# The residual of the Mamba stage: summed by DVE, or added by PE in the output projection's bank and copied by ACT

## The reference, cut to what matters

```
for i in range(4):                      # layers
    h = _rms(x, norm_w[i])
    xi, z = split(h @ W_in[i].T)        # 512 channels each
    xc = silu(conv4(xi) + conv_b[i])
    delta, Bm, Cm = split(xc @ W_x[i].T)
    delta = softplus(delta @ W_dt[i].T + b_dt[i])
    hs = scan(exp(delta * A), delta * xc * Bm)        # along the 512 tokens, 16 states
    y = sum_n(hs * Cm) + D[i] * xc
    out = (y * silu(z)) @ W_out[i].T                  # 512 x 256 a batch
    x = x + out                                       # the residual
```

## Time and profile before

| | |
|---|---|
| median of 3 runs | 4388.03 us (4382.81 to 4389.73) |
| the profiled execution's own time | 4372.04 us |
| its span | 4370.3 us |
| PE, DVE, ACT, POOL busy in the span | 85%, 70%, 53%, 54% |
| mean granted TensorE clock | 0.903 |
| Mamba stage, first product to last scan | 1796.4 to 3680.1 us |

### The profile page before, as it was taken

One profiled execution on the slowest core, in us unless ns is written; L12 is line 12 of the kernel. 1 busy time (PEld: TensorE's weight loads), 2 busy tenths in 40 slices (PEclk: granted clock), 3 DMA queues, 4 the chain that ended last, 5 costly groups with the idle time before them and its releaser, 6 DMA issues. The chain is left out here.

```text
span 4370.3 us, 51349 instructions
## 1 busy us (share of the span) xinstructions
PE 3704.9 (85%) x16520; PEld 1775.5 (41%) x16528; DVE 3046.8 (70%) x4067; ACT 2338.0 (53%) x4238; POOL 2360.4 (54%) x1238
## 2 busy tenths in 40 slices
PE   7979889889779995789898888899888977887786
PEld 3444444445369993222222222222222212454453
DVE  3566557556631113599999999999999997546547
ACT  4465446544622223676677767777677662333333
POOL 2354335434520003588988898889888884220220
PEclk9999999999989997798999989999999876788788
DMA  6000000000078883233434343334443352000000
GB/s 230 20 6 11 20 16 1 20 15 11 1 290 315 316 315 120 79 107 111 117 110 111 111 119 105 108 110 117 118 112 115 108 147 75 1 10 15 5 1 10
DMA packets 188417, 407.47 MB, mean 93 GB/s; under 512 B 30256, under 2 KB 76208, under 8 KB 182416
## 3 DMA queue, kind: packets, MB, share of 16 engines
q1 hardware_dynamic: 183232, 391.05, 28.4%
q0 software_dynamic: 4944, 13.51, 0.9%
HBM read 304.43 MB, written 32.90 MB: 77 GB/s over the span
## 5 line engine op out<-in xcount | busy, mean ns | idle before, releaser
L833 POOL TENSOR_TENSOR AR<-AR 128x1024 f32<-128x1024 f32 x512 | 1214.0, 2383 | 268.9 <-DVE AR L2080 256.9
L2080 DVE TENSOR_TENSOR_SCAN AR<-AR,PS 128x1024 f32<-128x1024 f32 x512 | 1169.9, 2285 | 20.1 <-POOL AR L833 4.6
L720 POOL TENSOR_TENSOR AR<-AR,rden 128x1024 f32<-128x1024 f32 x320 | 605.8, 1894 | 967.7 <-DVE rden L1808 900.4
L1139 ACT ACTIVATE AR<-AR,mcol 128x511 f32<-128x511 f32 x1024 | 671.8, 711 | 116.2 <-DVE AR L2080 114.0
L2072 DVE TENSOR_TENSOR PS<-AR,PS 128x1024 f32<-128x1024 f32 x512 | 628.6, 1228 | 57.0 <-PE PS L1569 41.1
L1584 PE MATMUL PS<-AR,upper 128*64 128x512 f32 x2048 | 636.9, 705 | 12.4 <-POOL AR L833 12.3
L1319 PE MATMUL PS<-ident,AR 128*128 128x128 f32 x2560 | 378.4, 295 | 108.4 <-POOL AR L720 92.0
L1319 PEld LDWEIGHTS PS<-ident,AR 128*128 128x128 f32 x2560 | 298.4, 150 | 356.1 <-POOL AR L720 222.6
L1569 PE MATMUL PS<-AR,sel 64*64 64x512 bf16 x1024 | 226.9, 440 | 179.8 <-DVE PS L2072 179.6
L1306 PE MATMUL PS<-AR 32*128 32x512 f32 (+1 forms) x1280 | 320.5, 718 | 44.4 <-ACT AR L897 11.5
L907 ACT ACTIVATE AR<-PS 128x512 f32<-128x512 f32 x320 | 189.8, 593 | 298.7 <-PE PS L1319 298.2
(11 more groups left out here) (264 smaller groups left out, 4824.2 us busy)
## 6 DMA issues: line engine op xcount, KB each, us to landing
AR<-mid_cs SPq DMA_DIRECT2D x1024, 128.0 KB, 3.0
AR<-in_xw SPq DMA_DIRECT2D x39, 3072.0 KB, 10.4
AR<-AR SPq DMA_DIRECT2D x512, 128.0 KB, 2.9
mid_xs<-AR SPq DMA_DIRECT2D x32, 512.0 KB, 7.9
AR<-mid_xs SPq DMA_DIRECT2D x39, 128.0 KB, 9.6
mid_ys<-AR POOLq DMA_DIRECT2D x39, 128.0 KB, 8.0
AR<-in_ctx SPq DMA_DIRECT2D x8, 512.0 KB, 6.5
AR<-in_mask SPq DMA_DIRECT2D x4, 1024.0 KB, 5.2
```

The costliest lines, as they stand in the source:

```text
L720: pool.tensor_tensor(probs[:, i % 4], probs[:, i % 4], rden[:, i % 4, :].rearrange("p (q o) -> p q o", o=1).to_broadcast([P, 2, 512]), ALU ...
L833: pool.tensor_tensor(m_HC[:, W % 3], m_H[:, W % 3, :].rearrange("p (c s) -> p c s", c=2), m_cb[:, W % 4:W % 4 + 1, :].to_broadcast([P, 2, ...
L1139: ins = act.activation(m_dA[:, W % 4, half, 1:512], m_dlr[:, G % 2, half, 1:512], ACT.Exp, scale=mcol[:, i // B, at:at + 1])
L2080: v.tensor_tensor_scan(m_H[:, W % 3, :], m_dA[:, W % 4].rearrange("p c s -> p (c s)"), PS[:, 4:6, :].rearrange("p c s -> p (c s)"), 0.0, A ...
```

## The change

PE adds a fifth product to each tile: the identity matrix (`ident`, there already) times the rows of x, accumulated into the same bank. The bank then holds x + out. ACT copies it over the rows (`rows_out`), as the first thing of its steps 11, 12, 13 and 16 behind `taken_y`, and counts `sh_ev` up in DVE's place. DVE's sums go. Behind the stage PE and ACT do the last item's four tiles, and DVE waits for the last of them.

```
+            def rows_out(i, t):                                              # ACT
+                src = taken(i, f"o{t}")
+                act.activation(R_all[:, (i - 1) % B, t, :], src[:, 0:D], ACT.Copy).then_inc(sh_ev, 1)
...
                     if i > 0 and 1 <= w < 3:
                         taken_y(i - 1, w - 1)
+                    if i > 0 and w - 1 in O_SLOT:
+                        rows_out(i, O_SLOT.index(w - 1))
                     if i + 1 < N_ITEM:
                         start_of(i, w)
...
             for hf in range(2):
                 taken_y(N_ITEM - 1, hf)
+            for t in range(T):
+                rows_out(N_ITEM, t)
...
                     for c in range(CI):                                      # PE
-                        ins = pe.matmul(bank[:, 0:D], m_sz[(i - 1) % 2][:, c, t * P:(t + 1) * P], mWout[:, c, :],
-                                        start=c == 0, stop=c == CI - 1)
-                    ins.then_inc(sh_ps, 1)
+                        pe.matmul(bank[:, 0:D], m_sz[(i - 1) % 2][:, c, t * P:(t + 1) * P], mWout[:, c, :],
+                                  start=c == 0, stop=False)
+                    pe.matmul(bank[:, 0:D], ident[:], R_all[:, (i - 1) % B, t, :], start=False, stop=True).then_inc(sh_ps, 1)
...
                                 PS[:, 6:7, :].to_broadcast([P, 2, 512]), ALU.mult).then_inc(d_bx, 1)    # DVE
-                if i > 0 and w - 1 in O_SLOT:
-                    residual(i, O_SLOT.index(w - 1))
...
-            def residual(i, t):
-
-                v.wait_ge(sh_ps, turn(i, f"o{t}") + 1)
-                r = R_all[:, (i - 1) % B, t, :]
-                v.tensor_tensor(r, PS[:, 7, 0:D], r, ALU.add).then_inc(sh_ev, 1)
...
-            for t in range(T):
-                residual(N_ITEM, t)
+            v.wait_ge(sh_ev, turn(N_ITEM, "o3") + 1)
```

## The result

| | before | changed |
|---|---|---|
| median | 4385.42 us (4382.38 to 4389.73, 4 runs) | 4441.81 us (4436.56 to 4443.66, 4 runs) |
| ratio | | 1.0126 (95% interval 1.0111 to 1.0141) |
| profiled execution: time, span | 4372.04, 4370.3 us | 4442.16, 4440.3 us |

The change makes the kernel 56 us slower. The forecast was 4449 us (4430 to 4478).

The account below looks back on a forecast made before the run. DVE, 97% busy, was taken to bound the selective scan. Thirteen items at 4.5 us, plus 3.5 for item 14, less 0.6 for item 15 and the tail, made 61.4 us; on 4388.03 that gave 4449 us, range 4430 to 4478.

Parts of the forecast that it names:

- DVE loses 0.205 us a residual: Selective scan, steps 11, 12, 13 and 16: each step without its residual sum gets 0.205 us shorter, 0.82 us an item.
- PE's product costs 0.46 us a tile and hides: Each of 64 output tiles: the identity product adds 0.46 us at full clock, hidden by PE's waiting except at the stage's end.
- ACT's copy takes 0.38 us: 64 copies of 128x256 out of the bank, 0.38 us each, bounds 0.2 and 0.60.
- The bank is handed back late, twice an item, and `spread` stands behind it: Items 1 to 13: o0's and o1's copies come late on ACT, delaying products 13 and 14; 4.06 us an item net.
- The clock adds 0.4 us an item: PE at half clock after idling before o1: 4.5 us an item taken instead of 4.06.
- item 14: No squares, so only the first wait: 3.5 us lost with the clock, ends 1.8 and 4.0.
- Rival 3: PE's clock stays low for o2 as well, 6.3 us an item: 85 us, 4473 us; 14%.
- Rival 2: Only the first wait counts, the squares' chain being shorter or overlapped: 23 us, 4411 us; 5%.
- Item 15 and the tail: End of the stage: item 15 gains 2.9 us, the last four tiles lose 2.3; together -0.6.
- the likeliest case: Late hand-over by ACT, twice in items 1 to 13: 53 to 66 us lost, 4441 to 4454 us; 76%.

Follow-up runs that it names:

- mended kernel: Changed kernel with o1 in the second half of o0's bank, one ACT copy for both, and the squares at step 6: 4358.96 us, ratio 0.9954.
- dose test: Changed kernel with the Silu over z cut to one element, so ACT's block ahead of o0's copy is shorter: 4410.79 us, ratio 1.0066.
- kernel with early squares: Changed kernel with ACT's squares and their two table loads moved from step 11 to step 6 of items 0 to 13: 4433.66 us, ratio 1.0105.

## Why the prediction was right, point by point

- *DVE loses 0.205 us a residual.* Right: in the mended kernel the steps lose 11.4 of the 11.5 us worked out for items 1 to 14. The estimate of 0.39 us from the Trainium skill's overhead ("Perfetto Trace Analysis", Optimizing Scalar/DVE Operations), weighed beside it, would have been 22 us. It is near the 417 ns that one sum shows in the trace, but not what a step gets shorter by without it.
- *PE's product costs 0.46 us a tile and hides.* The size is right: o0 of item 3 ends 5.12 us from product 10 (2210.88) where it ended at 4.69, so 0.43. That it hides is right only where the reader is patient. With DVE as reader it doesn't (16 us). With two tiles close together it hides, in the mended kernel. In the changed kernel it is part of the chain: without it, 9 us less.
- *ACT's copy takes 0.38 us.* 384 ns, 64 times.
- *The bank is handed back late, twice an item, and `spread` stands behind it.* Right in place, order and engine: o0's copy at 9.70, o1's start at 10.14 (10.13 worked out), o1's copy at 15.82 (15.9), product 14 at 19.13 (19.20).
- *The clock adds 0.4 us an item.* This term was oversized for items 1 to 13 and undersized for item 14. In nine of items 1 to 13 ACT's squares decide when o2 starts, and o1 may run slow under their cover; in the other four PE is only 0.2 to 0.4 us later. The steps cost 4.10 us an item (57.5 less 4.2 of item 14, over 13), not 4.5: 53 us where I had 58.5. Against the 4.06 worked out without any clock the clock added 0.04 us, not 0.4. In item 14, without squares, nothing covers it: 4.2 instead of 3.5, above the upper end of 4.0. The Trainium skill's rule ("TensorE: Matmul & The Clock Gate", HAM oscillation — how this bites in real kernels), that the group behind such a wait starts at half clock, fits o1 in part: behind 3.67 us of idle time its matmuls took 2.8 to 3.8 us instead of 1.99 in all 14 items, but in item 3 they started at full clock. It gives the product 13 and not the item. Behind the short waits of 0.47 to 0.93 us the tiles took 1.99 us each time.
- *Rival 3, o2 slow too.* Not in the changed kernel: o2 took 1.99 us in all 14 items, behind a second idle time of 0.93 us at most. It did happen in items 3 and 6 of the dose test, where o1 was fast and that time 2.35 us.
- *Rival 2, the first wait alone, 4411 us.* The kernel with early squares is that case, and it took 4434. My price of the first wait there left the slow clock out, while the forecast had it.
- *Item 15 and the tail.* Right in direction; how close the sizes came is partly luck. Item 15 gave -3.2 us where I had -2.9, but the unchanged kernel's item 15 took 121.7 us in one profile and 123.2 in the other. Behind the last product it is +1.7 where I had +2.3, and that part varies by 8 us without a change. From the start of the tail's first tile to the end of its last copy or sum the change costs 1.3 us (13.1 instead of 11.7). The tail's tiles follow each other at 2.90 us instead of 2.52, as ACT's copy and two hand-overs are 0.47 us, DVE's sum and two were 0.52, and the product adds 0.43:

```profile
3761.03 1.99 PE L1566 MATMUL PS<-AR 128*128 128x256 f32 x8 [0.47 <-ACT AR L1025]
3762.86 0.59 PE L1568 MATMUL PS<-AR,ident 128*128 128x256 f32 x2
3763.93 1.99 PE L1566 MATMUL PS<-AR 128*128 128x256 f32 x8 [0.47 <-ACT AR L1025]
```

- *4449 us.* 7 us too high. 5 are the clock term, and nearly 3 are the base: the forecast stood on a median of 4388.03 us, the result has 4385.42.
- *Two slips in the sums.* For item 14 at full clock 1.87 less a residual's 0.2 is 1.7, not 1.8, and the lower end of the likeliest case comes to 54 us, not 53. Neither changes the forecast.

## What to carry to other kernels
Work that moves to an engine with idle time takes over that engine's order. Ask where in its list the moved instruction stands, what the longest gapless block ahead of it is, and who is waiting for the buffer that it hands back. A share of 69% said nothing here; 6.3 us of Silu and table loads ahead of a 0.38 us copy cost 56 us in the end.

Two waits in one chain are not priced by adding them: removing the smaller gave some 8 us, and shortening the larger brought the smaller out at 2.35 us. And the move itself was sound: with two small results in one buffer and a block shifted, it gains 0.4% where it had lost 1.3%.

## What the runs showed of the hardware that I had not expected
The same idle time ahead of the same eight matmuls does not always have the same price. In the dose test 1.97 us was followed by 1.99 us of them in eight items and by 2.43 to 3.38 in six; 2.35 us was followed by 3.54 and 3.57 us in two items and by 1.99 in five. Behind 3.67 us they took 2.8 to 3.8 us in every item. Over the items the values nearly repeated from one profile of the changed kernel to the other (3.78 in items 2, 5, 7, 11 and 14 of both). The granted clock shows the direct reason: in item 3 of the changed kernel it fell only 1 us after o1 had started, in item 2 before o1 started. So the clock's price for one item is a range, and what decides when it falls is not settled here.

A DVE copy of 128x256 fp32 out of PSUM took 0.42 us, no less than the sum of it with a tile in SBUF.
